# Roots on another engine, a detour through DRAM and a new step order in the last stage of a four-layer graph network

## What is computed

```
L0: g = exp(c (e - offsets)^2), h = ssp(g W1 + b1), Wf = (h W2 + b2) * adj^2; y = sum_j rf_j Wf_ij; two dense layers
L1: hyperbolic attention. h = proj(mobius_add(proj(mobius_matvec(W, x)), bias))
    x_loc_ij = logmap(h_i, h_j);   a_ij = sigmoid(w2 . silu(att_w1 [x_self, x_loc_ij] + b1) + b2)
    s_i = sum_j a_ij x_loc_ij adj_ij;   two dense layers; out = proj(expmap(s, h)); x = expmap0(silu(logmap0(out)))
L2: (D^-1/2 adj D^-1/2 x) W + b
L3: messages = where(deg > 0, adj^T (x Ws) / max(deg, 1) + x Wr, 0);   [x, messages] W_upd
```

## Time and profile before

| | us |
|---|---|
| median of 3 runs | 2945.21 |
| the profiled execution | 2947.23 |
| its span, first to last instruction | 2945.1 |
| PE busy in the span | 2418.9 (82%) |
| DVE busy | 2180.2 (74%) |
| ACT busy | 2166.5 (74%) |
| POOL busy | 1784.1 (61%) |
| mean granted TensorE clock | 0.907 |

### The profile page before, as it was taken

How to read it: one execution, slowest core, us unless ns; L and a number is a source line. 1 busy time by engine, 2 the same in 40 slices (tenths; PEclk the granted TensorE clock), 3 DMA queues, 4 the chain that set the end, 5 groups by cost and what they waited for, 6 DMA issues and landing times. The chain is left out here.

```text
span 2945.1 us, 62968 instructions
## 1 busy us (share of the span) xinstructions
PE 2418.9 (82%) x25104; PEld 1176.0 (40%) x25104; DVE 2180.2 (74%) x3641; ACT 2166.5 (74%) x2140; POOL 1784.1 (61%) x1157
## 2 busy tenths in 40 slices
PE   4899999999999999999724867787868778686854
PEld 2333333333333333333322534454545445453433
DVE  5798998989899898989782537576767768573456
ACT  5888888888888888888533756666767768676643
POOL 0788998989889898989622444344435353443411
PEclk8999999999999999999866988798989989888976
DMA  8898998999899899999223546453745455464510
GB/s 219 185 202 194 200 200 195 199 197 197 197 199 201 195 200 195 199 197 198 51 61 67 109 85 119 73 119 67 133 67 98 99 100 100 88 110 75 87 46 18
DMA packets 311554, 408.15 MB, mean 139 GB/s; under 512 B 93024, under 2 KB 284128, under 8 KB 286176
## 3 DMA queue, kind: packets, MB, share of 16 engines
q1 hardware_dynamic: 311264, 404.14, 66.1%
HBM read 366.28 MB, written 33.55 MB: 136 GB/s over the span
## 5 line engine op out<-in xcount | busy, mean ns | idle before, releaser
L681 POOL TENSOR_TENSOR f_gate<-rfT,f_sq 128x1024 f32<-128x1024 f32 x512 | 1217.8, 2379 | 227.4 <-DVE f_prod L696 153.3
L614 PE MATMUL PS<-f_h,w_W2T 64*64 64x512 f32 x8192 | 998.9, 591 | 10.1 <-PE PS L614 1.9
L696 DVE SCALAR_TENSOR_TENSOR f_prod<-PS,b2l,f_gate 128x1024 f32<-128x1024 f32 x512 | 657.4, 1284 | 146.8 <-PE PS L614 111.0
L1332 POOL TENSOR_TENSOR a_outer<-a_by_i,a_by_j 128x256 f32<-128x256 f32 x512 | 347.7, 701 | 681.9 <-PE PS L1012 542.6
L1169 ACT ACTIVATE a_silu<-PS,c_att_b 128x1024 f32<-128x1024 f32 x512 | 542.4, 1109 | 296.0 <-PE PS L1012 295.3
L576 ACT ACTIVATE f_h<-PS,c_b 128x1024 f32<-128x1024 f32 x512 | 556.3, 1112 | 167.3 <-PE PS L596 166.5
L1012 PE MATMUL PS<-a_outer,a_rows 32*128 32x128 f32 x8192 | 412.7, 312 | 297.5 <-DMA a_rows<-hw_d 199.6
L688 DVE TENSOR_REDUCE yT<-f_prod 128x16 f32<-128x1024 f32 x512 | 618.7, 1209 | 0.0
L614 PEld LDWEIGHTS PS<-f_h,w_W2T 64*64 64x64 f32 x8192 | 340.9, 133 | 561.5 <-issue 438.1
L596 PE MATMUL PS<-f_gauss,W1two 64*64 64x512 f32 x4096 | 546.1, 595 | 7.1 <-ACT f_gauss L563 4.8
L1012 PEld LDWEIGHTS PS<-a_outer,a_rows 32*128 32x128 f32 x8192 | 337.7, 210 | 478.3 <-DMA a_rows<-hw_d 210.3
(11 more groups left out here) (253 smaller groups left out, 2238.4 us busy)
## 6 DMA issues: line engine op xcount, KB each, us to landing
f_gauss<-in_adj SPq DMA_DIRECT2D x128, 1024.0 KB, 11.6
f_sq<-adj_sq SPq DMA_DIRECT2D x256, 512.0 KB, 8.5
a_rows<-hw_d SPq DMA_DIRECT2D x1024, 64.0 KB
hw_d<-b_xc SPq DMA_DIRECT2D x16, 512.0 KB, 6.9
hw_d<-b_sq SPq DMA_DIRECT2D x16, 512.0 KB, 6.4
b_x<-in_x SPq DMA_DIRECT2D x8, 512.0 KB, 5.5
x_d<-b_x SPq DMA_DIRECT2D x8, 512.0 KB, 6.1
h_d<-b_h SPq DMA_DIRECT2D x8, 512.0 KB, 7.7
```

The source lines that it names most:

```text
L614: PE.matmul(post("message", c)[rows[b], n, :], W2T[rows[k], rows[fh]], hidden(c, n)[rows[k], b, :], start=not second, stop=bool(second)).t ...
L681: GP.tensor_tensor(by_pair(GATE[c % GATE_BUFS][:]), rf, by_pair(squares), ALU.mult).then_inc(s_gate, 1)
L696: V.scalar_tensor_tensor(PR[c % PR_BUFS][:], post("message", c).rearrange("p b n -> p (b n)"), b2l[:, c % 2:c % 2 + 1], GATE[c % GATE_BUFS ...
L1332: GP.tensor_tensor(OUTER[s % OUTER_BUFS][:, :, u * A_BLOCK:(u + 1) * A_BLOCK, :], BY_I[g % 2][:, :, tl, (2 * k + u) * A_BLOCK:(2 * k + u + ...
```

## The change

Only `flow_stage` and its tables change.

1. *i terms.* `U` is stored to a new DRAM tensor `u_d` in two transfers (one for each half of 32 columns), SP waits for them, and four loads of 64 KB fill BY_J, whose layout is turned from [tile, block] to [block, tile].
2. *Column roots.* All ACT square roots but that of the pair chain (L1234) go. POOL computes x^-1/2 with an integer first guess and three Newton steps (`root`, 14 to 16 small instructions), and the root as x times it. DVE's clamps and reciprocals behind the roots go; MIN_SQ bounds the square from below instead.
3. *Normed ReLUs.* In mix and last the mean is subtracted by POOL in one pass over 128x1024 into gH, ACT squares it into gU, DVE reduces it, and after the inverse root DVE computes max(gH, 0) times the inverse root in one pass. Before, DVE had 8 passes with accumulation and ACT 8 ReLUs.
4. *Small ones.* The attention weight is (1 + tanh) with the factor 1/2 moved to the evacuation of s (scale=0.5); one DVE pass instead of two.
5. *Order.* All due numbers of all engines are new.

```
 FILLS = {
-    "lead": (("y0", 32.0625), ("y1", 35), ("t0", 41), ("t1", 43), ("m0", 45), ("m1", 46)),
-    "pair": (("h0", 9), ("h1", 11), ("g", 13), ("y", 21), ("r0", 23), ("r1", 25), ("r2", 29), ("r3", 31)),
-    "mix": (("u0", 18), ("u1", 18.0625), ("v0", 31.0625), ("v1", 31.125), ("s0", 32), ("s1", 35.0625),
-             ("a0", 35.125), ("a1", 36), ("z0", 38.0625), ("z1", 38.125)),
-    "last": (("l0", 15), ("l1", 17), ("k0", 19), ("k1", 27), ("t0", 37), ("t1", 38), ("p0", 40), ("p1", 42),
-             ("p2", 42.0625), ("p3", 47), ("q0", 49), ("q1", 51), ("e0", 51.0625), ("e1", 55)),
+    "lead": (("y0", 35), ("y1", 35), ("t0", 45.5), ("t1", 46.9375), ("m0", 46.9375), ("m1", 46.9375)),
+    "pair": (("h0", 23.5625), ("h1", 23.5625), ("g", 23.5625), ("y", 23.5625), ("r0", 23.5625),
+             ("r1", 23.5625), ("r2", 23.5625), ("r3", 25.9375)),
+    "mix": (("u0", 13.1875), ("u1", 13.1875), ("v0", 27.5625), ("v1", 27.5625), ("s0", 27.5625),
+             ("s1", 27.5625), ("a0", 27.5625), ("a1", 27.5625), ("z0", 28.0625), ("z1", 28.0625)),
+    "last": (("l0", 15.25), ("l1", 15.25), ("k0", 15.25), ("k1", 17.8125), ("t0", 51.1875), ("t1", 51.1875),
+             ("p0", 57.1875), ("p1", 57.1875), ("p2", 57.1875), ("p3", 57.1875), ("q0", 57.1875),
+             ("q1", 57.1875), ("e0", 57.1875), ("e1", 57.1875)),
 }
...
@@ sp_program
         def pair(g):
             nodes = slice(g * GT, (g + 1) * GT)
-            yield 33.0625
+            yield 25.25
             taken(SP, number["pair", g, "r3"])
...
-            yield 49
+            yield 48.5625
             SP.wait_ge(b["vt"], g + 1)
...
             SP.wait_ge(b["U"], g + 1)
+            for half_of in range(2):
+                SP.dma_start(d["u"][g % 2, half_of], U[g % 3][:, :, half_of * 32:half_of * 32 + 32]).then_inc(d_ust, 16)
+            SP.wait_ge(d_ust, (g + 1) * 2 * 16)
             for c in range(4):
-                for i in range(A_BLOCKS):
-                    first = c // 2 * NODES + i * A_BLOCK
-                    SP.dma_start(BY_J[g % 2][rows_by_i(c, 0), :, i, :, :].rearrange("p t j m -> p t (j m)"),
-                                 U[g % 3][first:first + A_BLOCK, :, c % 2 * 32:c % 2 * 32 + 32]).then_inc(d_u[g % 2], 16)
+                by_i = d["u"][g % 2, c % 2, c // 2 * NODES:(c // 2 + 1) * NODES].rearrange("(b i) t m -> i b (t m)", i=A_BLOCK)
+                SP.dma_start(BY_J[g % 2][rows_by_i(c, 0)].rearrange("p b t j m -> p b (t j m)"), by_i
+                             ).then_inc(d_u[g % 2], 16)
...
@@ gp_program
+        def root(own, x, inverse, half_x, sq, norms, done, g):
+            own.before(GP)
+            GP.tensor_scalar(inverse.bitcast(I32), x.bitcast(I32), -0.5, MAGIC, ALU.mult, ALU.add).then_inc(*own.gives())
+            GP.tensor_scalar(half_x, x, -0.5, None, ALU.mult).then_inc(*own.gives())
+            for step in range(3):
+                own.before(GP)
+                GP.tensor_tensor(sq, inverse, inverse, ALU.mult).then_inc(*own.gives())
+                own.before(GP)
+                GP.tensor_tensor(sq, sq, half_x, ALU.mult).then_inc(*own.gives())
+                own.before(GP)
+                GP.tensor_scalar(sq, sq, 1.5, None, ALU.add).then_inc(*own.gives())
+                own.before(GP)
+                GP.tensor_tensor(inverse, inverse, sq, ALU.mult).then_inc(
+                    *own.gives(*((done, g) if step == 2 and norms is None else ())))
+            if norms is not None:
+                own.before(GP)
+                GP.tensor_tensor(norms, x, inverse, ALU.mult).then_inc(*own.gives(done, g))
...
@@ gp_program
         def mix(g):
...
+            yield 8.4375
+            GP.wait_ge(f["n1"], g + 1)
+            at_least(own_m, sF("n1"))
+            root(own_m, sF("n1"), sF("in1"), sF("half"), sF("sq"), sF("sn1"), f["sqrt1"], g)
+            yield 34.3125
+            GP.wait_ge(f["n2"], g + 1)
+            root(own_m, sF("n2"), sF("in2"), sF("half"), sF("sq"), sF("sn2"), f["sqrt2"], g)
...
@@ act_program
         def last(g):
...
-            for k in range(4):
-                yield (13.0625, 13.125, 13.1875, 15)[k]
-                A.wait_ge(f["bias"], g + 1)
-                relu(k, f["relu"])
+            A.wait_ge(f["xb"], 3 * g + 1)
+            A.activation(gU, gH, ACT.Square).then_inc(f["csq"], 1)
...
@@ dve_program
         def last(g):
...
-            tt(s("bias"), s("bias"), s("rstd"), MU, gives=(f["bias"], g))
+            stt(gH, gH, 0.0, of_nodes(s("rstd")), MA, MU, gives=(f["relu"], g))
```

More of the change, by code:

```diff
@@ L789, in flow_stage @@
     BY_I = [sb(f"a_by_i{n}", [P, 2, GT, NODES]) for n in range(2)]
-    BY_J = [sb(f"a_by_j{n}", [P, GT, A_BLOCKS, 2, BLOCK]) for n in range(2)]
+    BY_J = [sb(f"a_by_j{n}", [P, A_BLOCKS, GT, 2, BLOCK]) for n in range(2)]
     OUTER = [sb(f"a_outer{n}", [P, 2, BLOCK, BLOCK]) for n in range(OUTER_BUFS)]
@@ L958, in mix @@
             SP.wait_ge(d_h, (g + 1) * 16)
-            before(SP, f["var"], g)
+            before(SP, f["mean"], g)
             SP.dma_start(fH[:], d["h"][:, nodes, :]).then_inc(d_adj, 16)
-            yield 9.125
+            yield 16
             SP.wait_ge(s_tanh, g + 1)
@@ L1278, in mix @@
-            A.wait_ge(f["n3"], g + 1)
-            A.activation(sF("sn3"), sF("n3"), ACT.Sqrt).then_inc(f["sqrt3"], 1)
-            yield 67
-            A.wait_ge(f["clamp"], g + 1)
+            yield 56.875
+            A.wait_ge(f["sqrt3"], g + 1)
             A.activation(sF("sc"), sF("sn3"), ACT.Tanh).then_inc(f["tanh3"], 1)
         def last(g):
-            num, s = numbers("last", g), sG(g)
-            def relu(k, done):
-                for t in (2 * k, 2 * k + 1):
-                    end = A.activation(gH[:, t, :], fXs[g % 2][:, t, :], ACT.Relu, scale=s("rstd")[:, t:t + 1],
-                                       bias=s("bias")[:, t:t + 1])
-                end.then_inc(done, 1)
@@ L1293, in last @@
-            for k in range(4):
-                yield (13.0625, 13.125, 13.1875, 15)[k]
-                A.wait_ge(f["bias"], g + 1)
-                relu(k, f["relu"])
+            num = numbers("last", g)
+            yield 1.4375
+            if g:
+                for name in ("p2", "p3", "q0", "q1"):
+                    taken(A, number["last", g - 1, name])
+            A.wait_ge(f["xb"], 3 * g + 1)
+            A.activation(gU, gH, ACT.Square).then_inc(f["csq"], 1)
             for h in range(2):
-                yield (15.0625, 17)[h]
+                yield (15.5, -47.5)[h]
@@ L1299, in last @@
                 evacuate(num[f"l{h}"], half(gU, h))
-            for k in range(4):
-                yield (31.1875, 33, 33.0625, 33.125)[k]
-                A.wait_ge(f["bias3"], g + 1)
-                relu(k, f["relu3"])
+            yield 39.75
+            A.wait_ge(f["xb"], 3 * g + 3)
+            A.activation(gU, gH, ACT.Square).then_inc(f["csq"], 1)
             for h in range(2):
-                yield (37, 39)[h]
+                yield (55.375, 48.625)[h]
                 evacuate(num[f"t{h}"], half(gU, h))
@@ L1322, in gp_program, with at_least @@
         GP.wait_ge(s_hb, 2)
+        own_l, own_m = Order(o_lp), Order(o_mp)
+        def root(own, x, inverse, half_x, sq, norms, done, g):
[15 more added lines that the diff above has]
+                GP.tensor_tensor(norms, x, inverse, ALU.mult).then_inc(*own.gives(done, g))
+        def at_least(own, x):
+            GP.tensor_scalar(x, x, MIN_SQ, None, ALU.max).then_inc(*own.gives())
         def outer(s):
@@ L1392, in mix @@
             GP.tensor_tensor(fXC[:], fH[:], fUU[:], ALU.mult).then_inc(f["hu"], 1)
-            yield 60
+            yield 8.4375
[5 more added lines that the diff above has]
+            root(own_m, sF("n2"), sF("in2"), sF("half"), sF("sq"), sF("sn2"), f["sqrt2"], g)
+            yield 46.6875
             GP.wait_ge(f["cu"], g + 1)
             GP.tensor_tensor(fUU[:], fUU[:], of_nodes(sF("cu")), ALU.mult).then_inc(f["uc"], 1)
+            yield 55.875
+            GP.wait_ge(f["n3"], g + 1)
+            at_least(own_m, sF("n3"))
+            root(own_m, sF("n3"), sF("in3"), sF("half"), sF("sq"), sF("sn3"), f["sqrt3"], g)
         def last(g):
-            yield 20
-            GP.wait_ge(f["relu"], 4 * g + 4)
-            GP.tensor_tensor(fXs[g % 2][:], fXs[g % 2][:], row(rows["L2_b"]), ALU.add).then_inc(f["xb"], 1)
+            X = fXs[g % 2]
+            yield -79.875
+            if g:
+                for h in range(2):
+                    taken(GP, number["last", g - 1, f"e{h}"])
+            GP.wait_ge(f["mean"], g + 1)
+            GP.tensor_tensor(gH, X[:], of_nodes(sG(g)("bias")), ALU.add).then_inc(f["xb"], 1)
+            yield -118.125
+            GP.wait_ge(f["xb"], 3 * g + 1)
+            GP.tensor_tensor(X[:], X[:], row(rows["L2_b"]), ALU.add).then_inc(f["xb"], 1)
+            yield 26.8125
+            GP.wait_ge(f["mean3"], g + 1)
+            GP.tensor_tensor(gH, X[:], of_nodes(sG(g)("bias")), ALU.add).then_inc(f["xb"], 1)
```

(9 more changed lines are left out.)

358 lines of the change are left out of this document (170 added, 188 removed).

## The result

The changed kernel takes **2803.09 us** (median of 4 runs, 2801.47 to 2805.9) against 2946.26 (median of 4) for the kernel before, measured beside it: a ratio of **0.9514**, 95% interval [0.9497, 0.9530]. The forecast was 2880, so the change brings 143 us where 65 were expected. The profiled execution of the changed kernel has a span of 2804.1 us and a mean granted clock of 0.938.

The account below looks back on a forecast made before the run. Waits and step order, no full engine, set the time. Slot terms sum to -6.8 of 162 us: six periods -41, first and eighth slots -8 and -6, run-in -15, run-out +5, together -65, giving 2880; range 2800 to 2985.

Parts of the forecast that it names:

- Its own sign of being wrong: Attention slots of the last stage: the prediction called itself wrong if they shrank by over 12 us.
- i terms, -17.7: Slot boundary: shorter i-term transfers remove PE's 14.1 us row-load wait, plus 3.6 for a higher clock afterwards.
- SP's step ahead of the eighth tile, +3: SP's queue: i-term transfers ahead of the eighth tile's row loads delay them, +3 us per slot, between 0 and 8.
- ACT's table loads, -5.3: ACT: three roots that brought their own table-load pairs go, 1.75 us each, -5.3 us per slot.
- POOL's roots, +5: POOL, in order: three roots hold outer products of sets only two ahead, +5 us per slot, bounds 0 and 20.
- POOL's calls: Small POOL instructions in the roots: 0.2 us each, 16 us of POOL per slot, 3.3 per root.
- The second rival: POOL's roots hold the outer products: at 0.45 us per small call, slots of 167 us, 2988 us; chance 0.14.
- ReLUs, -2.8: ACT: sixteen ReLUs become two squares, so ACT loses 5.6 us, half on the path, -2.8 per slot.
- The order, +22 and -6: PE's fills in bursts cost +22 us per slot (12 to 32); more room for late steps gives -6 (0 to -10).
- The floor of 145: Per slot: 102 us of attention plus bursts, table changes and other stalls; the new order cannot go below 145.
- Run-out +5: After the last slot: three POOL roots on the path, slower than roots on ACT, +5 us.
- The first rival: Well balanced: bursts stand where PE would wait anyway, slots reach 145 us, about 2807 us; chance 0.26.

Follow-up runs that it names:

- e4: The kernel before with i terms through DRAM, roots on POOL and whole-tile ReLUs, in the old order, without the merged attention weight: 2878.32 us, ratio 0.9796.
- e1: The kernel before with only the i terms sent through DRAM, old order: 2832.02 us, ratio 0.965.
- e5: The changed kernel with the 32 direct transfers of the i terms put back, new order kept: 2935.94 us, ratio 1.000.
- e2: The kernel before with only the roots moved to POOL, near their old places: 2928.79 us, ratio 0.9967.
- e7: The changed kernel with all square roots on ACT again, with DVE's clamps and reciprocals, new order kept: 2892.75 us, ratio 0.9866.
- e6: The changed kernel with six Newton steps in each POOL root instead of three: 2922.44 us, ratio 0.996.
- e3: The kernel before with only the normed ReLUs as whole-tile passes, old order: 2961.83 us, ratio 1.0086.
- e16: The changed kernel with two Newton steps per POOL root instead of three, measured in one call with the changed kernel: 2769.43 us, ratio 0.9432.
- e12: The changed kernel with DVE's two large reciprocals of the pair chain replaced by multiplications by one: 2794.15 us, ratio 0.9523.

## Why the prediction was wrong

The time lay in the range, the direction was right, but the size was less than half of what came. Its own sign of being wrong, slots shorter by over 12 us, came up: a full slot lost 19.0. Two errors of opposite sign stand behind that, and e4 separates them. The parts without the order (i terms, table loads, ReLUs, POOL's roots) were put at -20.8 per slot and brought 8.6 (162.5 to 153.9). The order (+22, -6, and +3 and -5 for SP's steps) was put at +14 and brought 10.4 more (153.9 to 143.5). By its own steps, per slot:

- **i terms, -17.7:** the mechanism is right, the size too large. e1 alone has 157.1 to 144.8 between Tanhs, 12.3 less (13.0 in full slots). That is what the row-load waits at the boundary had (13.0), and of the 3.6 added for the clock nothing shows. In the new order the same step is worth 16.4 (e5), and that its value depends on where it stands (3.5% or 4.9%) I didn't see. The run-in and first slot, 23 forecast, gained 34.4 in e1 and 21 in the changed kernel. The hop was taken as 4.8, from the store of the attention values; the two stores landed in 3.0, so 5.9 us in place of 9.4.
- **SP's step ahead of the eighth tile, +3:** too much. With the short block that tile's first products wait 1.1 us (2247.26). In e5 the same place with the long block costs all that the rest gains.
- **ACT's table loads, -5.3, and POOL's roots, +5:** together -0.3 forecast, -4.1 in the old order (e2, 162.5 to 158.4). Which of the two was off by how much there isn't shown. In the new order the roots on ACT cost 16.5 (e7), with 11 loads more, not 6. An estimate by the drain of 1.38 us for each load (the Trainium skill, ScalarE: Activation LUTs, "What ACT_TABLE_LOAD costs") was -13 for the three pairs. ACT's timeline of the changed kernel doesn't bear the drain out: the load at 2203.33 follows the SiLU that ends at 2203.31, and the root starts at 2204.63, 0.02 behind its 1.28.
- **POOL's calls:** 0.2 us each was right (0.20 to 0.30), partly by luck: the 2.15 us that the line went through is a mean of passes of 1.89 and of 2.93, and through 1.89 the same line gives 0.30. What was wrong is how much of them is on the path, 0.18 to 0.27 us of slot per call and not a third of it. The second rival's mechanism is real, PE waited 25 us for held products in e6, and at 0.2 us per call it doesn't decide.
- **ReLUs, -2.8:** wrong in the old order (e3: +0.9%). Taking them alone back out of the new order wasn't tried.
- **The order, +22 and -6: this is the step that failed.** The sign is wrong: +16 expected, and the new order on the same parts takes 10.4 off a full slot (8.6 between Tanhs: e4 148.7, changed 140.1). The +22 came from 26 of 38 fills in four bursts, each bare fill 1.16, less "3.5 for what such pairs cost now", and rested on the line that a fill alone in its set hides. The line is true of the earlier trace rows; what is wrong is that it stands for the old order. There 23 of 32 sets hold fills, 10 of them several, and some hold one whose input comes late. They cost 42.3 us per slot in e4, and in the kernel before 41.4, or 35.5 without the row-load wait. The four bursts of the new order (sets 7, 11, 13 with 14, and 28, counted from 0) cost 23.4 us, near the 25.5 worked out before the 3.5 came off; with its other sets with fills, which the prediction didn't cost, it is 33.7. So the new places were priced nearly right, and the old ones at 3.5 where they cost over 35.
- **The floor of 145:** the four full slots have 141.5 to 146.7, their mean, 143.5, is 1.5 below it. The floor was a sum of stalls one after the other; that some of ACT's work stands beside PE's bursts would explain it, and isn't shown.
- **Run-out +5:** e2 alone shows it (+8.0). In the changed kernel it is -1.3; the order there took it back.

The first rival ("well balanced", 2807) has the time, 4 us off, and half of the mechanism. The chain through the roots, in which DVE waits for POOL, does bound the slot (e16), though not how much DVE has to do: 5.3 us less of its work in the pair chain bring nothing (e12). But the bursts aren't hidden in waits. They replace dearer fills. The weight of 0.26 was too low, and the reason against it, that a burst delays SiLUs on the path, held for the old fills just as well.

## What to carry to other kernels

Before a new order is costed, cut the bound engine's timeline into its periods and sum, for the order that is there, what each kind of period costs above a lone one; a single hidden instance doesn't stand for the rest. The gains of parts aren't a sum: taking the queue's long block away is what lets the order bring anything (e5), and where roots moved off ACT bring 0.3% in one order, putting them back costs 3.5% in another, in which each brings its own table loads. Count the loads at the new places too. Newton steps on an engine with room are cheap only off the path; count them first.

## What was not expected of the hardware

- A small POOL instruction (128x8, fp32) takes 0.20 to 0.25 us in most groups, with 0.08 between two dependent ones; DVE does the same in about 0.19. Three times the elements (128x24) take 0.24 to 0.42. The Trainium skill, GPSIMD Engine Reference, "Elementwise — side-by-side cycle accounting", puts the dispatch of a DVE instruction at some 156 ns and gives POOL's no figure; DVE's 0.19 agrees with it, and POOL's 0.20 is hardly more.
- How long a pass over 128x1024 takes depends on what the other of POOL and DVE does at the time. From the kernel before, POOL's `f_uu` pass alone and beside a DVE multiplication of two SBUF operands (2808.25, 1.22 us), then DVE's add to `b_h` alone and beside POOL's `b_x` pass (2.36 us from 1732.55):

```profile
2028.40 1.89 POOL L1395 TENSOR_TENSOR f_uu<-f_uu,f_small 128x1024 f32<-128x1024 f32 x1
...
2808.29 2.93 POOL L1395 TENSOR_TENSOR f_uu<-f_uu,f_small 128x1024 f32<-128x1024 f32 x1 [2.91 <-DVE f_small L1420]
...
1498.10 1.23 DVE L1420 TENSOR_TENSOR b_h<-b_h,b_sq 128x1024 f32<-128x1024 f32 x1
...
1732.63 3.36 DVE L1420 TENSOR_TENSOR b_h<-b_h,b_sq 128x1024 f32<-128x1024 f32 x1 [6.96 <-POOL b_sq L1350]
```

All eight `f_uu` passes of the changed kernel meet the multiplication (2.93), before it was two of eight. The add met `b_x` in six of eight groups before; in the changed kernel seven meet outer products, and take 1.53. In these rows the one that started second took longer, by nearly what was left of the other.

- Two stores of 128 KB in pieces of 128 bytes landed in 3.0 us (median), sooner than the one of 256 KB with 4.8.
